# Token rows of 192 features instead of 256 columns, and a split that writes low parts to the other half of the partitions

## The chip, the cores and the metric

One core of one Trainium2 chip runs the whole program in one launch. The metric is the device time of the launch in microseconds (us), lower is better. All instructions of the five engines (TensorE or PE, VectorE or DVE, ScalarE or ACT, GpSimd or POOL, SyncE or SP) are placed by hand, and waits are semaphores that the program sets itself.

## The reference

A small language-model tower in float32: 8 sequences of 256 tokens, 192 features per token. An embedding with layer norm, four transformer layers with banded attention, then four residual blocks on normed input. Cut to its core:

```python
def layer_norm(x, s, b): ...
for l in range(4):
    q = heads(h @ Wq[l] + bq[l]); k = heads(h @ Wk[l] + bk[l]); v = heads(h @ Wv[l] + bv[l])
    a = band_attention(q, k, v, mask)          # each token sees 64 tokens to either side
    h = layer_norm(h + a @ Wo[l] + bo[l], ln1_s[l], ln1_b[l])
    f = gelu(h @ W1[l] + b1[l])                # 192 -> 768
    h = layer_norm(h + f @ W2[l] + b2[l], ln2_s[l], ln2_b[l])
h = h + channel_attention(layernorm(h))        # 8 heads of 24 channels, softmax over channels
h = h + best_expert_of_4(layernorm(h))         # argmax gate, each expert 192 -> 768 -> 192
h = h + full_attention(layernorm(h))           # 12 heads, 8 x 256 tokens
h = h + best_2_of_8_experts(layernorm(h))      # softmax over the two best scores
```

The output is h, 2048 x 192. The attention mask is all ones in these inputs, and there are 2048 tokens = 16 tiles of 128.

## The kernel before

**Tiles.** A token tile is 128 tokens, one per partition. `h` (the residual stream) and `xn` (normed or attention rows) are `[128, 16, 256]`: columns 0 to 191 are the features, and columns 192 to 255 hold features 128 to 191 a second time. The 16 tiles go in four groups of four (`GT = 4`). `hb` holds h plus the next bias, 192 wide.

**Turn and split.** Each product contracts over features, so a tile's features have to lie on partitions. PE transposes a tile in two turns of 128 columns (`pe_transpose`, L431; L1446 for the experts, L2098 for the gates). The second turn therefore has features 128 to 191 twice: on partitions 0 to 63 and again on 64 to 127. A value is carried as a rounded part (fp32r) and the rest, its low part. ACT copies both turns rounded into `xx[:, 0:2]` (`act_split`, L652; L1502). DVE then makes the low parts (`dve_split`; the same pair stands at L1539/L1540):

```python
nc.vector.tensor_tensor(xx[:, 2, tk], ps[:, 0:P], xx[:, 0, tk].bitcast(F32), ALU.subtract)       # L765
nc.vector.scalar_tensor_tensor(xx[:, 1, tk], in0=xx[:, 1, tk].bitcast(F32), scalar=lo_rows[:, :],
                               in1=ps[:, P:2 * P], op0=ALU.mult, op1=ALU.add)                     # L766
```

`lo_rows` is 0 on partitions 0 to 63 and -1 on 64 to 127. So L766 puts the unrounded turn on the lower half of `xx[:, 1]` (where the output's rounding makes it the high part) and turns the upper half into low parts. It ends the split and lets PE go on (`xx_ready`). The weights match: `second` has rows 128 to 191 of the weights on both halves, `second_lo` their low parts on partitions 0 to 63 and zeros above. A product is five matmuls (`pe_features` L449 to L453, `pe_tokens` L459 to L463, the experts' L1459 to L1463).

**Who writes rows.** DVE writes h at the end of each layer norm: as two instructions per tile, 128 columns each, since columns 128 to 255 are features 128 to 191 written twice (`dve_affine` L938 and L941 after L932; `dve_norm_step` L854 and L857 after L848, which is the same norm cut into steps that stand between the pairs of the attention loop). `dve_normalise` (L912) writes `xn` in two instructions per tile, 192 and 64 wide. POOL's `pool_scale` writes attention rows and, on every other call, a copy of 64 columns (L1044). The experts read rows of `x_rows` in DRAM, 256 wide, by an indirect transfer (L1386) into `rows_in`, a piece of the `xn` buffer.

**Order of the work.** 0 to 62 us: loads, embedding gather, first norm. Then four layers of an attention part (96 pairs of heads: scores on PE, maximum L792 on DVE, exponentials L685 on ACT, transposes L563 on PE, high part L698 on ACT, low part L799 on DVE, values L584 to L586 on PE) and a tail (output product, norm, 192 to 768 to 192, norm), whose end overlaps with the next layer's opening. Then channel attention (1080 to 1201), gates (1201 to 1236), 11 expert tiles of 256 slots (to 1346), sums and norm (to 1380), full attention (1400 to 1545), tail and router (to 1642), 23 expert tiles (to 1840), last sums and output. DVE's order in a loop is fixed by `dve_step` and `dve_attention`, in a tail by `dve_tail` and the table `TURNED`.

Of the kernel before, what the change touches and what calls it, by code (L numbers as in the profile page):

```python
# [119 lines left out]
def build_tower(nc, a, out, stop=None):  # L120
    ctx = ExitStack()
    with ctx:
# [9 lines left out]
        columns = sb("columns", [P, 3])  # L132
        lo_rows, q_scale, neg_in = columns[:, 0:1], columns[:, 1:2], columns[:, 2:3]
# [41 lines left out]
        def over(n, *dims):  # L175
# [21 lines left out]
        early = [flat(xn[:, 8 + 3 * j:11 + 3 * j, :], "p a n -> p (a n)").bitcast(BF16)  # L197
                 .rearrange("p (a n) -> p a n", a=3) for j in range(2)] + [pieces[2]]
        spare = flat(xn[:, :, :], "p t d -> p (t d)")
        raw_e = [spare[:, 2 * FF * j:2 * FF * (j + 1)].rearrange("p (a n) -> p a n", a=2) for j in range(2)]  # L200
        rows_in = spare[:, 4 * FF:4 * FF + 4 * 256].rearrange("p (s n) -> p s n", s=4)
# [59 lines left out]
        padded = sig("weight_rows_padded", base=0)  # L261
# [88 lines left out]
        x_rows = nc.dram_tensor("x_rows", (NT * P, 256), F32, kind="Internal").ap()  # L350
# [73 lines left out]

        def pe_transpose(pe, it, s, t, src, ready, turn, n, inside=False):

            pe.wait_ge(ready.sem, ready.at(turn, n))
            pe.wait_ge(xx_ready.sem, xx_ready.at(it, s if inside else s - 1))
            o = turn_at(t, inside)
            for c in range(2):  # L430
                last = nc.tensor.transpose(o[:, c * P:c * P + P],  # L431
                                           src[:, t, c * P:c * P + P], ident[:, :])
            last.then_inc(xt_done.sem, 1)
# [308 lines left out]
        def dve_step(dve, ch, it, p, banded, tile):  # L742

            if p and step(p - 1, banded):
# [3 lines left out]
                elif kind == "tile":  # L748
                    tile(a, True)
                elif kind == "att":  # L750
                    dve_split(dve, it, turned(1, a), a, True)
                elif kind == "out":
                    dve.wait_ge(hb_ready.sem, hb_ready.at(it, normed(2, a) - 2 * NT))
                    dve.wait_ge(o_done.sem, o_done.at(it, a + 1))
                    nc.vector.tensor_tensor(h[:, a, 0:D], bank[BM[0]][:, 0:D], hb[:, a, :], ALU.add)\
                        .then_inc(o_read.sem, 1)
# [5 lines left out]
        def dve_split(dve, it, s, t, inside=False):  # L762
# [3 lines left out]
            nc.vector.scalar_tensor_tensor(xx[:, 1, tk], in0=xx[:, 1, tk].bitcast(F32), scalar=lo_rows[:, :],  # L766
                                           in1=ps[:, P:2 * P], op0=ALU.mult, op1=ALU.add)\
# [70 lines left out]
        def dve_norm_step(dve, ch, it, i, n, g, w):  # L838
# [8 lines left out]
            if i % 2 == 0:  # L847
                last_mark[0] = ch.mark(nc.vector.scalar_tensor_tensor(  # L848
                    hb[:, t, :], in0=h[:, t, 0:D], scalar=mv[:, t, 0:1], in1=ln_s[:, w, :],
                    op0=ALU.subtract, op1=ALU.mult))  # L850
            else:
                twice = lambda x: x.unsqueeze(1).to_broadcast([P, 2, D2])
# [22 lines left out]
        def dve_residual(dve, ch, it, half, g, hb_n=None):  # L875

            for t in range(GT * g, GT * g + GT):
# [11 lines left out]
                nc.vector.tensor_tensor(h[:, t, 0:D], ps[:, 0:D], hb[:, t, :], ALU.add)\  # L889
                    .then_inc(read.sem, 1)  # L890

        def dve_stats(dve, ch, it, half, g, read):

            c = []
            for i in range(GT):
                if read:
                    dve.wait_ge(read.sem, read.at(it, GT * g + i + 1))
                c.append(ch.mark(nc.vector.bn_stats(stats[:, (GT * g + i + NT - GT) % NT, :], h[:, GT * g + i, 0:D])))
# [28 lines left out]
        def dve_affine(dve, ch, it, n, g, w):  # L927
# [3 lines left out]
            for t in range(GT * g, GT * g + GT):  # L931
                c.append(ch.mark(nc.vector.scalar_tensor_tensor(  # L932
                    hb[:, t, :], in0=h[:, t, 0:D], scalar=mv[:, t, 0:1], in1=ln_s[:, w, :],
                    op0=ALU.subtract, op1=ALU.mult)))
            twice = lambda x: x.unsqueeze(1).to_broadcast([P, 2, D2])
            for i, t in enumerate(range(GT * g, GT * g + GT)):
                ch.done(c[i])
                nc.vector.scalar_tensor_tensor(  # L938
                    h[:, t, 0:P], in0=hb[:, t, 0:P], scalar=rstd[:, t, 1:2], in1=ln_b[:, w, 0:P],
                    op0=ALU.mult, op1=ALU.add)  # L940
                nc.vector.scalar_tensor_tensor(  # L941
                    h[:, t, P:2 * P].rearrange("p (a n) -> p a n", a=2), in0=twice(hb[:, t, P:D]),
                    scalar=rstd[:, t, 1:2], in1=twice(ln_b[:, w, P:D]), op0=ALU.mult, op1=ALU.add)                    .then_inc(h_ready.sem, 1)
# [46 lines left out]
        def pool_hb(pool, it, n, g, row):  # L990
            for t in range(GT * g, GT * g + GT):
                pool.wait_ge(h_ready.sem, h_ready.at(it, n + t % GT))
                nc.gpsimd.tensor_tensor(hb[:, t, :], h[:, t, 0:D], row[:, :], ALU.add)\
# [28 lines left out]
        def pool_weights(ch, w, c1, c0=0):  # L1022
# [7 lines left out]
            return nc.gpsimd.tensor_tensor(second_lo[0:D2, 0:c1], raw[0:D2, 1, c],  # L1030
                                           second[0:D2, 0:c1].bitcast(F32), ALU.subtract)

        def pool_scale(pool, it, f):
# [9 lines left out]
            if half:  # L1043
                last = nc.gpsimd.tensor_tensor(o[:, :, HEADS:, :], x[:, :, 2:6, :], r[:, :, 2:6, :], ALU.mult)  # L1044
# [234 lines left out]
        def dve_xc_out(dve, b):  # L1279
            dve.wait_ge(xc_o_done.sem, xc_o_done.at(0, b + 1))  # L1280
            for i in range(2):
                t = 2 * b + i
                dve.wait_ge(hb_ready.sem, hb_ready.at(LAYERS, normed(2, t) - 2 * NT))
                nc.vector.tensor_tensor(h[:, t, 0:D], bank[2][:, i * D:i * D + D], hb[:, t, :], ALU.add)\
# [151 lines left out]
        def pe_tiles(pe, m):  # L1436
            first, end = span(m)[0], span(m)[-1] + 1

            def turn(G):

                pe.wait_ge(e_rows_in[G % 2].sem, 32 * (G // 2 + 1))
                for s in range(2):
                    if G > first:
                        pe.wait_ge(e_x_ready.sem, 2 * G + s - 1)
                    for c in range(2):
                        last = nc.tensor.transpose(bank[BX[s]][:, c * P:c * P + P],  # L1446
                                                   rows_in[:, 2 * (G % 2) + s, c * P:c * P + P], ident[:, :])
                    last.then_inc(e_turned.sem, 1)
# [74 lines left out]
        def dve_tiles(dve, m):  # L1523
            first, end = span(m)[0], span(m)[-1] + 1

            def low(G, i):

                dve.wait_ge(e_hi_ready.sem, 2 * G + i + 1)
                rows = slice(0, P if i == 0 else D2)
                hi, lo, second, second_lo = (wa, wb)[G % 2]  # L1530
                nc.vector.tensor_tensor((lo, second_lo)[i][rows, 0:FF], raw_e[G % 2][rows, i, :],
                                        (hi, second)[i][rows, 0:FF].bitcast(F32), ALU.subtract)\
                    .then_inc(e_lo_ready.sem, 1)

            def split(G):
                for s in range(2):
# [3 lines left out]
                    nc.vector.scalar_tensor_tensor(xx[:, 1, tk], in0=xx[:, 1, tk].bitcast(F32), scalar=lo_rows[:, :],  # L1540
                                                   in1=ps[:, P:2 * P], op0=ALU.mult, op1=ALU.add)\
# [84 lines left out]
        def _(sp):  # L1626
            for dst, src in ((ident, "ident"), (lo_rows, "lo_rows"), (q_scale, "q_scale"),
# [9 lines left out]
            sp.dma_start(xn[:, 0:8, :].bitcast(I32), a["mask_BS_i1_0"].unsqueeze(0).to_broadcast([P, B, S]))\  # L1637
# [75 lines left out]
            if stop is None:  # L1713
                o = out.rearrange("(t p) d -> p t d", p=P)
                for g in range(NG):
                    tg = slice(GT * g, GT * g + GT)
                    sp.wait_ge(sum_ready.sem, sum_ready.at(0, g + 2))
                    sp.dma_start(o[:, tg, :], h[:, tg, 0:D]).then_inc(out_done.sem, 16)
                sp.wait_ge(out_done.sem, 16 * NG)
            if stop == "tok":  # L1720
                sp.wait_ge(h_ready.sem, h_ready.at(L, 0))
                sp.dma_start(out.rearrange("(t p) d -> p t d", p=P), h[:, :, 0:D]).then_inc(out_done.sem, 16)
# [3 lines left out]
        def _(pool):  # L1726
# [8 lines left out]
            for t in range(NT):  # L1735
                pool.indirect_dma_start(out=h[:, t, 0:D], out_offset=None, in_=a["L0_tok_emb_word"],
# [3 lines left out]
            pool.wait_ge(const_in.sem, 16 * 8)  # L1740
# [81 lines left out]
            for g in range(NG):  # L1822
# [3 lines left out]
                if g == 0:  # L1826
                    pool.wait_ge(rows_bo.sem, rows_bo.at(L + 1, 16))
                    pool.wait_ge(sum_ready.sem, sum_ready.at(0, 1))
                    for t in range(NT):
                        nc.gpsimd.tensor_tensor(hb[:, t, :], h[:, t, 0:D], row_bo[:, :], ALU.add)\  # L1830
# [13 lines left out]
        def _(act):  # L1844
            for s in (xh_ready, qf_ready, exp_done, pad_ready, hi_ready, f_ready, xc_qk_ready, xc_v_ready, xc_e_ready, xc_y_ready, r_ready, g2_exp):
                s.start(act)
            act.wait_ge(const_in.sem, 16 * 8)
# [401 lines left out]
```

## Time and profile before

| | |
|---|---|
| device time, 3 runs | 1876.59, 1876.82, 1877.55 us (median 1876.82) |
| span of the profiled execution | 1874.5 us; 2.3 us of the median lie around it |
| mean granted TensorE clock | 0.895 of full speed |
| PE busy | 1483.1 us (79%), 13098 matmuls |
| DVE busy | 1247.8 us (67%), 3542 instructions |
| ACT busy | 977.2 us (52%), 2392 instructions |
| POOL busy | 808.0 us (43%), 1177 instructions |
| DMA | 178.26 MB in 144317 packets, 95 GB/s |

The profiled execution has no separate device time, so the time beside its span is the median of the three runs. A busy engine isn't necessarily the bound: the program passes through stages in which one engine after another ends last. The chain of waits, followed back from the last instruction, covers the time from 836 us to the end; before that the stages repeat (layers 1 to 3 run as layer 4 does).

### The profile page before, as it was taken

What the parts mean: (1) busy time and instruction counts of PE and PEld (TensorE: products, weight loads), DVE (VectorE), ACT (ScalarE), POOL (GpSimd) and SP (SyncE); (2) the same over time, 40 slices, a digit from 0 to 9 for tenths busy, and PEclk for the clock granted to TensorE, in tenths of its full rate; (3) what the DMA queues carried; (4) which work ended last, traced back from release to release, by engine and by line L of the source; (5) the groups of instructions that cost most, each with busy time, mean ns of one, the idle gap of its engine ahead of it and who ended that gap; (6) DMA issues with size and microseconds to landing.
All of it is one profiled execution on the core that took longest, in us unless ns stands there. A gap on an engine that the chain in (4) does not pass through costs nothing.

```text
span 1874.5 us, 42615 instructions
## 1 busy us (share of the span) xinstructions
PE 1483.1 (79%) x13098; PEld 1235.0 (66%) x13098; DVE 1247.8 (67%) x3542; ACT 977.2 (52%) x2392; POOL 808.0 (43%) x1177
## 2 busy tenths in 40 slices
PE   0589889798897997998988759759668887499992
PEld 0367678677676776776767648449646766389992
DVE  4788966788767888668896652433379896434344
ACT  0378733688434885348873223225348882155550
POOL 6577333684235762247733310124356521144440
PEclk9899989899899997999998968669869996599996
DMA  4666101743005550035610000147534511257765
GB/s 105 176 149 127 36 1 33 170 86 84 1 5 138 108 121 2 1 70 140 128 33 1 1 14 1 45 138 224 173 89 100 112 22 45 97 175 237 225 212 179
DMA packets 144317, 178.26 MB, mean 95 GB/s; under 512 B 22096, under 2 KB 106128, under 8 KB 143952
## 3 DMA queue, kind: packets, MB, share of 16 engines
q1 hardware_dynamic: 136784, 158.18, 32.9%
q0 software_dynamic: 7296, 17.18, 2.8%
q8 instruction: 117, 1.92, 0.5%
q14 instruction: 120, 0.98, 0.2%
HBM read 132.96 MB, written 42.34 MB: 94 GB/s over the span
## 4 chain that ended last, share of the span: by engine, by line
PE 31%; DVE 14%; issue 4%; DMA 2%; ACT 2%; POOL 2%; SPq 0%; DVEq 0%; POOLq 0%; ACTq 0%
PE bank L1473 7%; DVE ptl L799 4%; PE bank L1459 2%; DVE neg_max L792 2%; PE bank L645 1%; DVE xn L912 1%; PE bank L563 1%; PE bank L1460 1%; PE bank L1463 1%; PE bank L1461 1%; PE bank L1462 1%; PE bank L1217 1%; DMA xn<-y_rows 1%; PE bank L431 1%; PE bank L584 1%
## 5 line engine op out<-in xcount | busy, mean ns | idle before, releaser
L685 ACT ACTIVATE prob<-bank,neg_max 128x192 f32<-128x192 f32 (+1 forms) x960 | 406.9, 437 | 109.3 <-DVE neg_max L792 97.0
L792 DVE TENSOR_REDUCE neg_max<-bank 128x2 f32<-128x384 f32 (+1 forms) x480 | 274.3, 572 | 99.0 <-PE bank L544 91.4
L799 DVE TENSOR_TENSOR ptl<-bank,pth 128x384 f16<-128x384 f32 (+1 forms) x480 | 275.5, 574 | 4.6 <-ACT pth L698 4.0
L563 PE MATMUL bank<-ident,prob 128*128 128x128 f32 x1536 | 268.4, 288 | 0.0
L698 ACT ACTIVATE pth<-bank 128x384 f16<-128x384 f32 (+1 forms) x480 | 244.3, 509 | 9.3 <-PE bank L563 9.2
L652 ACT ACTIVATE xx<-bank 128x256 fp32r<-128x256 f32 x256 | 95.5, 386 | 196.0 <-PE bank L431 192.0
L544 PE MATMUL bank<-kx,qx 96*128 96x192 bf16 (+1 forms) x960 | 168.1, 257 | 1.1 <-DVE xx L766 1.1
L563 PEld LDWEIGHTS bank<-ident,prob 128*128 128x128 f32 x1536 | 162.9, 143 | 0.1
L584 PE MATMUL bank<-v,pth 128*128 128x33 bf16 x1152 | 138.4, 180 | 21.2 <-DVE ptl L799 18.0
L645 PE MATMUL bank<-w,fbuf 128*128 128x192 f32 x768 | 140.7, 327 | 2.0 <-DVE h L889 2.0
L734 ACT ACTIVATE fbuf<-bank,b 128x512 f32<-128x512 f32 x96 | 65.8, 687 | 146.5 <-PE bank L453 146.4
L542 PE MATMUL bank<-mask,ident 128*128 128x384 bf16 x384 | 130.6, 340 | 8.9 <-issue 7.3
L986 POOL TENSOR_SCALAR rstd<-mv 128x4 f32<-128x4 f32 x52 | 12.5, 240 | 289.4 <-DVE mv L902 283.4
L645 PEld LDWEIGHTS bank<-w,fbuf 128*128 128x128 f32 x768 | 128.6, 190 | 12.2 <-issue 5.2
L586 PE MATMUL bank<-v,ptl 128*128 128x33 bf16 x1152 | 136.5, 178 | 0.0
L585 PE MATMUL bank<-v,pth 128*128 128x16 bf16 x1152 | 132.9, 171 | 0.0
L584 PEld LDWEIGHTS bank<-v,pth 128*128 128x128 f16 x1152 | 99.4, 96 | 43.5 <-DVE ptl L799 42.8
L1396 POOL DMA_INDIRECT y_rows<-vf,mask x68 | 70.9, 1043 | 131.9 <-DVE vf L1550 116.0
L431 PE MATMUL bank<-ident,h 128*128 128x128 f32 x256 | 53.6, 315 | 83.8 <-DVE h L941 48.9
L544 PEld LDWEIGHTS bank<-kx,qx 96*128 96x128 bf16 x960 | 95.2, 101 | 36.0 <-issue 4.6
L1473 PE MATMUL bank<-w,fbuf 128*128 128x192 f32 x552 | 112.9, 329 | 0.0
L1515 ACT ACTIVATE fbuf<-bank,b 128x256 f32<-128x256 f32 x138 | 64.0, 473 | 89.4 <-PE bank L1463 60.4
(295 smaller groups left out, 4522.5 us busy)
## 6 DMA issues: line engine op xcount, KB each, us to landing
xn<-in_e_seg SPq DMA_DIRECT2D x34, 768.0 KB
w<-in_e_w SPq DMA_DIRECT2D x23, 576.0 KB
qk_rows<-fbuf SPq DMA_DIRECT2D x128, 96.0 KB, 2.3
qx<-qk_rows SPq DMA_DIRECT2D x35, 288.0 KB, 4.0
kx<-qk_rows SPq DMA_DIRECT2D x35, 288.0 KB, 5.8
qk_rows<-w SPq DMA_DIRECT2D x80, 96.0 KB, 2.3
qx<-qk_rows SPq DMA_DIRECT2D x35, 192.0 KB, 4.6
kx<-qk_rows SPq DMA_DIRECT2D x35, 192.0 KB, 5.2
```

Source lines behind the costliest of these rows:

```text
L542: nc.tensor.matmul(o, ident_bf, mask[:, 2 * b:2 * b + 2, :], start=True, stop=False)
L544: last = nc.tensor.matmul(o[:, qt, :], qx[0:ROWS, b % 3, hd, qt * P:qt * P + P], kx[0:ROWS, b % 3, hd, keys(qt, banded)], start=not banded ...
L563: last = nc.tensor.transpose(bank[BT[p % 2]][:, c * P:c * P + P], probs_at(p, banded, c * P, P), ident[:, :])
L584: nc.tensor.matmul(o, pth[:, p % 3, w], v[sums], start=first, stop=False)
L585: nc.tensor.matmul(o[third], pth[:, p % 3, w], v[lows], start=False, stop=False)
L586: return nc.tensor.matmul(o, ptl[:, p % 2, w], v[sums], start=False, stop=stop)
L645: last = nc.tensor.matmul(bank[BY[t]][:, 0:D], fbuf[:, (n - 2) % 4, t * P:t * P + P], w2[:, c, :], start=(c == 0), stop=(c == FC - 1))
L685: nc.scalar.activation(probs_at(p, banded, qt * n, n), scores_at(p, n)[:, qt, :], ACT.Exp, bias=neg_max[:, b % 2, hd, qt:qt + 1], scale=1. ...
L698: nc.scalar.activation(pth[:, p % 3, 0:n], bank[BT[p % 2]][:, 0:n], ACT.Copy).then_inc(hi_ready.sem, 1)
L792: nc.vector.tensor_reduce(neg_max[:, b % 2, hd, :], scores_at(p, D if banded else S), AX.X, ALU.max, negate=True).then_inc(max_ready.sem, 1)
L799: nc.vector.tensor_tensor(ptl[:, p % 2, 0:n], bank[BT[p % 2]][:, 0:n], pth[:, p % 3, 0:n], ALU.subtract)\
L1473: last = nc.tensor.matmul(bank[BY[2 * (G % 2) + s]][:, 0:D], fbuf[:, n % 4, s * P:s * P + P], w2_e[G % 3][:, c, :], start=(c == 0), stop=( ...
```

## The change

`h`, `xn`, `x_rows` and `rows_in` become 192 wide, without the second copy. The first turn takes columns 0 to 127 as before, the second columns 64 to 191, so that features 128 to 191 come out on partitions 64 to 127 (and features 64 to 127 on 0 to 63, unused). ACT rounds both turns as before. The split's second instruction subtracts on 64 partitions: it reads 64 to 127 and writes the low parts to partitions 0 to 63. `second_lo` then has low parts on all 128 partitions, so its zero rows and their two memsets go; so do `lo_rows` and its load. Norm outputs become one instruction of 192 columns per tile.

```diff
-        h = sb("h", [P, NT, 256])
-        xn = sb("xn", [P, NT, 256])
+        h = sb("h", [P, NT, D])
+        spare = sb("spare", [P, NT * 256])[:, :]
+        xn = spare[:, 0:NT * D].rearrange("p (t d) -> p t d", d=D)
...
-        x_rows = nc.dram_tensor("x_rows", (NT * P, 256), F32, kind="Internal").ap()
+        x_rows = nc.dram_tensor("x_rows", (NT * P, D), F32, kind="Internal").ap()
...
+        def turn_rows(o, rows):
+
+            nc.tensor.transpose(o[:, 0:P], rows[:, 0:P], ident[:, :])
+            return nc.tensor.transpose(o[:, P:2 * P], rows[:, D - P:D], ident[:, :])
...
             nc.vector.tensor_tensor(xx[:, 2, tk], ps[:, 0:P], xx[:, 0, tk].bitcast(F32), ALU.subtract)
-            nc.vector.scalar_tensor_tensor(xx[:, 1, tk], in0=xx[:, 1, tk].bitcast(F32), scalar=lo_rows[:, :],
-                                           in1=ps[:, P:2 * P], op0=ALU.mult, op1=ALU.add)\
+            nc.vector.tensor_tensor(xx[0:D2, 1, tk], ps[D2:P, P:2 * P], xx[D2:P, 1, tk].bitcast(F32), ALU.subtract)\
                 .then_inc(xx_ready.sem, 1)
...
-                nc.vector.scalar_tensor_tensor(
-                    h[:, t, 0:P], in0=hb[:, t, 0:P], scalar=rstd[:, t, 1:2], in1=ln_b[:, w, 0:P],
-                    op0=ALU.mult, op1=ALU.add)
-                nc.vector.scalar_tensor_tensor(
-                    h[:, t, P:2 * P].rearrange("p (a n) -> p a n", a=2), in0=twice(hb[:, t, P:D]),
-                    scalar=rstd[:, t, 1:2], in1=twice(ln_b[:, w, P:D]), op0=ALU.mult, op1=ALU.add)\
-                    .then_inc(h_ready.sem, 1)
+                nc.vector.scalar_tensor_tensor(
+                    h[:, t, :], in0=hb[:, t, :], scalar=rstd[:, t, 1:2], in1=ln_b[:, w, :],
+                    op0=ALU.mult, op1=ALU.add).then_inc(h_ready.sem, 1)
...
-                for dst, src in ((slice(0, D), slice(0, D)), (slice(D, 256), slice(P, D))):
-                    last = nc.vector.tensor_scalar(xn[:, t, dst], h[:, t, src], mv[:, t, 0:1],
-                                                   rstd[:, t, 1:2], ALU.subtract, ALU.mult)
-                last.then_inc(xn_ready.sem, 1)
+                nc.vector.tensor_scalar(xn[:, t, :], h[:, t, :], mv[:, t, 0:1],
+                                        rstd[:, t, 1:2], ALU.subtract, ALU.mult).then_inc(xn_ready.sem, 1)
...
-            return nc.gpsimd.tensor_tensor(second_lo[0:D2, 0:c1], raw[0:D2, 1, c],
-                                           second[0:D2, 0:c1].bitcast(F32), ALU.subtract)
+            return nc.gpsimd.tensor_tensor(second_lo[:, 0:c1], raw[:, 1, c],
+                                           second[:, 0:c1].bitcast(F32), ALU.subtract)
...
-            if half:
-                last = nc.gpsimd.tensor_tensor(o[:, :, HEADS:, :], x[:, :, 2:6, :], r[:, :, 2:6, :], ALU.mult)
...
-            for dst, src in ((ident, "ident"), (lo_rows, "lo_rows"), (q_scale, "q_scale"),
+            for dst, src in ((ident, "ident"), (q_scale, "q_scale"),
                              (neg_in, "neg_in"), (pad_keys, "pad_keys")):
                 sp.dma_start(dst[:, :], a[src]).then_inc(const_in.sem, 16)
...
-            nc.vector.memset(wa[3][D2:P, :].bitcast(F32), 0.0)
-            nc.vector.memset(wb[3][D2:P, :].bitcast(F32), 0.0).then_inc(padded.sem, 1)
```

The experts' turn, split and low parts (L1446, L1539/L1540, L1531) change in the same way, and the gates' product reads `wg[D2:P, 1]` in place of `wg[0:D2, 1]`. No wait of the kernel is moved; PE's instructions are as many as before. In the changed kernel the split's pair is L766/L767, the norm step's one instruction L853, the affine's L930, the normalise L906.

Two places on DVE show what is replaced. In the first attention loop (a norm step of the opening behind a split, between two pairs), before:

```order
L763 REGISTER_ALU
L765 TENSOR_TENSOR xx<-bank,xx 128x128
L766 SCALAR_TENSOR_TENSOR xx<-xx,columns,bank 128x128
L99 ISA
L854 SCALAR_TENSOR_TENSOR h<-hb,rstd,ln_b 128x128
L857 SCALAR_TENSOR_TENSOR h<-hb,rstd,ln_b 128x128
L791 REGISTER_ALU
L792 TENSOR_REDUCE neg_max<-bank 128x2
```

and now:

```order
L764 REGISTER_ALU
L766 TENSOR_TENSOR xx<-bank,xx 128x128
L767 TENSOR_TENSOR xx<-bank,xx 64x128
L99 ISA
L853 SCALAR_TENSOR_TENSOR h<-hb,rstd,ln_b 128x192
L791 REGISTER_ALU
L792 TENSOR_REDUCE neg_max<-bank 128x2
```

The place of the split and of the step is the same; the second instruction of the split has half the partitions, and the step is one instruction instead of two.

At the channel attention's input, where DVE makes statistics, normalises the second group of four tiles and splits the first, before (the pair L912 comes four times, once per tile):

```order
L902 BN_AGGR mv<-stats 128x2 x4
L912 TENSOR_SCALAR xn<-h,mv,rstd 128x192
L912 TENSOR_SCALAR xn<-h,mv,rstd 128x64
...
L765 TENSOR_TENSOR xx<-bank,xx 128x128
L766 SCALAR_TENSOR_TENSOR xx<-xx,columns,bank 128x128
```

and now:

```order
L897 BN_AGGR mv<-stats 128x2 x4
L906 TENSOR_SCALAR spare<-h,mv,rstd 128x192 x4
L766 TENSOR_TENSOR xx<-bank,xx 128x128
L767 TENSOR_TENSOR xx<-bank,xx 64x128
```

Four instructions stand where eight did, ahead of the same four splits.

## Rows read from the trace of the kernel before

**Rows 1.** Stages: stretch, length, busy PE, PEld, DVE, ACT, POOL, PEclk, DMA, GB/s.

```profile
850.00:975.00 125.00, 110.73 (x1437) 88.27 (x1433) 110.95 (x293) 104.33 (x295) 77.38 (x123) 0.99 0.45 96
975.00:1080.00 105.00, 83.22 (x464) 71.56 (x462) 69.17 (x252) 28.01 (x54) 33.77 (x54) 0.88 0.01 4
1080.00:1102.00 22.00, 9.04 (x32) 4.64 (x32) 17.97 (x78) 5.92 (x16) 3.91 (x6) 0.50 0.06 14
1346.00:1380.00 34.00, 8.72 (x28) 5.92 (x28) 25.76 (x84) 4.63 (x9) 9.68 (x15) 0.60 0.33 101
1642.00:1840.00 198.00, 193.06 (x1333) 182.35 (x1331) 78.45 (x185) 107.45 (x228) 88.86 (x87) 0.98 0.64 200
```

**Rows 2.** DVE by line and form: busy, mean ns; idle before, releaser.

```profile
L766 DVE SCALAR_TENSOR_TENSOR xx<-xx,columns,bank 128x128 fp32r<-128x128 f32 x256 | 86.5, 338 | 0.0
L765 DVE TENSOR_TENSOR xx<-bank,xx 128x128 fp32r<-128x128 f32 x256 | 73.2, 286 | 52.7 <-ACT xx L652 52.2
...
L912 DVE TENSOR_SCALAR xn<-h,mv,rstd 128x192 f32<-128x192 f32 x64 | 24.2, 379 | 0.6 <-POOL rstd L987 0.6
L912 DVE TENSOR_SCALAR xn<-h,mv,rstd 128x64 f32<-128x64 f32 x64 | 19.6, 307 | 0.0
...
L1531 DVE TENSOR_TENSOR wa_second_lo<-xn,wa_second 64x768 fp32r<-64x768 f32 x17 | 16.8, 986 | 6.3 <-issue 3.3 <-ACT wa_second L1495 3.0
...
L1531 DVE TENSOR_TENSOR wa_lo<-xn,wa_hi 128x768 fp32r<-128x768 f32 x17 | 16.3, 959 | 50.0 <-ACT wa_hi L1495 45.5 <-issue 4.5
```

**Rows 3.** Timeline of SP, first issues: start, length.

```profile
0.73 0.39 SPq L1629 DMA_DIRECT2D ident<-in_ident  x1
1.18 0.42 SPq L1629 DMA_DIRECT2D columns<-in_lo_rows  x1
```

**Rows 4.** Timeline of DVE, layer norm of a group, without and with POOL beside it.

```profile
264.06 1.41 DVE L932 SCALAR_TENSOR_TENSOR hb<-h,mv,ln_s 128x192 f32<-128x192 f32 x4 [1.69 <-POOL rstd L987]
...
267.05 0.68 DVE L941 SCALAR_TENSOR_TENSOR h<-hb,rstd,ln_b 128x128 f32<-128x128 f32 x1
...
267.91 0.68 DVE L941 SCALAR_TENSOR_TENSOR h<-hb,rstd,ln_b 128x128 f32<-128x128 f32 x1
...
277.47 0.35 DVE L938 SCALAR_TENSOR_TENSOR h<-hb,rstd,ln_b 128x128 f32<-128x128 f32 x1
277.74 0.35 DVE L941 SCALAR_TENSOR_TENSOR h<-hb,rstd,ln_b 128x128 f32<-128x128 f32 x1
```

**Rows 5.** Chain of waits, channel attention's input: start, length, what.

```profile
1080.02 2.14 DVE xn L912 x8
...
1085.56 0.20 DVE xx L765
1085.76 0.27 DVE xx L766
...
1086.86 0.39 ACT xx L652
...
1087.27 0.29 DVE xx L765
1087.57 0.25 DVE xx L766
```

**Rows 6.** Chain of waits, other stretches that the change touches.

```profile
845.65 0.34 DVE xx L766
...
974.34 0.26 DVE h L854
974.60 0.26 DVE h L857
...
1238.64 6.96 DMA xn<-x_rows,mask
...
1373.36 4.56 DVE xn L912 x16
...
1593.02 0.27 DVE xx L766
```

More of the change, by code:

```diff
@@ L429, in pe_transpose @@
             o = turn_at(t, inside)
[L430 to L433, printed above, removed]
+            turn_rows(o, src[:, t, :]).then_inc(xt_done.sem, 1)
         def pe_turn(pe, it, k, g, read):
@@ L888, in dve_residual @@
                     ps, read = bank[BY[t % 4]], y_read
-                nc.vector.tensor_tensor(h[:, t, 0:D], ps[:, 0:D], hb[:, t, :], ALU.add)\
+                nc.vector.tensor_tensor(h[:, t, :], ps[:, 0:D], hb[:, t, :], ALU.add)\
                     .then_inc(read.sem, 1)
@@ L992, in pool_hb @@
                 pool.wait_ge(h_ready.sem, h_ready.at(it, n + t % GT))
-                nc.gpsimd.tensor_tensor(hb[:, t, :], h[:, t, 0:D], row[:, :], ALU.add)\
+                nc.gpsimd.tensor_tensor(hb[:, t, :], h[:, t, :], row[:, :], ALU.add)\
                     .then_inc(hb_ready.sem, 1)
@@ L1444, in turn @@
                         pe.wait_ge(e_x_ready.sem, 2 * G + s - 1)
[L1445 to L1448, printed above, removed]
+                    turn_rows(bank[BX[s]], rows_in[:, 2 * (G % 2) + s, :]).then_inc(e_turned.sem, 1)
             def up(n):
@@ L1528, in low @@
                 dve.wait_ge(e_hi_ready.sem, 2 * G + i + 1)
-                rows = slice(0, P if i == 0 else D2)
                 hi, lo, second, second_lo = (wa, wb)[G % 2]
-                nc.vector.tensor_tensor((lo, second_lo)[i][rows, 0:FF], raw_e[G % 2][rows, i, :],
-                                        (hi, second)[i][rows, 0:FF].bitcast(F32), ALU.subtract)\
+                nc.vector.tensor_tensor((lo, second_lo)[i][:, 0:FF], raw_e[G % 2][:, i, :],
+                                        (hi, second)[i][:, 0:FF].bitcast(F32), ALU.subtract)\
                     .then_inc(e_lo_ready.sem, 1)
@@ L1829, in _ @@
                     for t in range(NT):
-                        nc.gpsimd.tensor_tensor(hb[:, t, :], h[:, t, 0:D], row_bo[:, :], ALU.add)\
+                        nc.gpsimd.tensor_tensor(hb[:, t, :], h[:, t, :], row_bo[:, :], ALU.add)\
                             .then_inc(hb_ready.sem, 1)
@@ L1846, in _ @@
                 s.start(act)
-            act.wait_ge(const_in.sem, 16 * 8)
+            act.wait_ge(const_in.sem, 16 * 7)
             def first_split(it):
@@ L1927, in _ @@
             dve.wait_ge(mask_in.sem, 32)
-            km = xn[:, 8:16, :]
-            ch.link(nc.vector.tensor_copy(km, xn[:, 0:8, :].bitcast(I32)))
-            ch.link(nc.vector.tensor_scalar(xn[:, 0:8, :], km, 0.0, -1.0, ALU.is_gt, ALU.add))
-            ch.link(nc.vector.tensor_scalar(km, xn[:, 0:8, :], -NEG_IN, None, ALU.mult))
+            km_in, km = [spare[:, j * B * S:(j + 1) * B * S].rearrange("p (b s) -> p b s", s=S) for j in range(2)]
+            ch.link(nc.vector.tensor_copy(km, km_in.bitcast(I32)))
+            ch.link(nc.vector.tensor_scalar(km_in, km, 0.0, -1.0, ALU.is_gt, ALU.add))
+            ch.link(nc.vector.tensor_scalar(km, km_in, -NEG_IN, None, ALU.mult))
             for t in range(NT):
@@ L1991, in _ @@
                     dve_merge(dve, ch, 0, g)
-                    added = ch.mark(nc.vector.tensor_tensor(h[:, tg, 0:D], h[:, tg, 0:D], hb[:, tg, :], ALU.add))
+                    added = ch.mark(nc.vector.tensor_tensor(h[:, tg, :], h[:, tg, :], hb[:, tg, :], ALU.add))
                 if g == NG:
@@ L2096, in _ @@
                             pe.wait_ge(gx_ready.sem, t - 1)
-                        for c in range(2):
-                            last = nc.tensor.transpose(bank[BX[t % 2]][:, c * P:c * P + P],
-                                                       xn[:, t, c * P:c * P + P], ident[:, :])
-                        last.then_inc(gx_done.sem, 1)
+                        turn_rows(bank[BX[t % 2]], xn[:, t, :]).then_inc(gx_done.sem, 1)
                 if g >= 2:
@@ L2170, in lay_out @@
     o["ident"] = np.eye(P, dtype=np.float32)
-    o["lo_rows"] = -(row >= 64).astype(np.float32)[:, None]
     o["q_scale"] = np.where(row < 64, DH ** -0.5, 1.0).astype(np.float32)[:, None]
```

56 lines of the change are left out of this document (24 added, 32 removed).

## The prediction

> **What bounds the kernel now.** I read the busy times by stage first, then VectorE's groups by line and form, then the chain of waits through the stretches that the change touches. The stages don't share one bound [rows 1]. In the experts' stretch PE is busy for 193.06 of 198 us: nothing that DVE or POOL saves there shows. In a layer's attention (850 to 975) PE has 110.73 of 125 us and DVE 110.95, and they hand work to each other in a ring, so what DVE saves counts in part. In a tail PE leads (83.22 of 105), with gaps at each turn. In the two norms without matrix work, 1080 to 1102 and 1346 to 1380, DVE is busy for 17.97 of 22 and 25.76 of 34 us and PE for 9: there nearly every DVE instruction lies on the path. So the change has to be costed as DVE time, stage by stage.
>
> Two views of DVE are to be kept apart. The mean of an instruction is from its start to its end; the next one starts before that end. The split's first instruction has a mean of 286 ns [rows 2], yet where it isn't held up its successor starts 0.20 us behind it, and the pair repeats after 0.20 + 0.26 = 0.46 us [rows 5]. Pitch, not mean, is what an instruction costs in a row of them; the mean counts only where someone waits for its end.
>
> **Terms that save.** All are against the profiled execution, which goes with the median of 1876.8 us.
>
> Start: one transfer fewer is issued by SP ahead of the token list. Issues stand 0.45 us apart (0.73 to 1.18) [rows 3], and the gather hangs on the token list. −0.5. The two memsets run while DVE waits for that list: 0.
>
> Normalise, 64 tiles: eight instructions for four tiles take 2.14 us on the chain [rows 5], so a tile costs 0.515 with the last one's end taken off. The 192-wide one is 379 − 307 = 72 ns longer than the 64-wide one [rows 2]; split so, the pitches are 0.295 and 0.22, and 0.22 us per tile go. Where they lie on the path: the channel attention's input, 16 tiles, −3.5. The gates' 16 tiles, −1.7, half of it, since after the second group PE and ACT's loop over the groups sets the pace. The norm of 1346 to 1380, −2.3: of the first two groups most is given back to a wait for PE's turn and ACT's copy, the last sixteen instructions (4.56 us) [rows 6] lose their eight at the end. Last tail, 8 of 16 tiles, −1.7. Sum −9.2.
>
> Norm output, first norm of the program: two 128-wide instructions cost 0.27 each (277.47, 277.74) [rows 4], one 192-wide of the same kind (1.41 − 0.09) / 4 = 0.33. So −0.20 per tile, twelve tiles not covered by statistics and POOL: −2.4. Where POOL adds the bias at the same time, a tile takes 0.86 us (267.05 to 267.91) [rows 4] and the saving may be larger.
>
> Norm steps in the attention loops: 32, each a pair of 0.26 us [rows 6], less 0.20 each. By the chain of layer 4 half of them are on the path: 16 × 0.20 = −3.2.
>
> Norms in tails: the last group of layer 4, where nothing else is left, −1.2 (4 × 0.30, between 0.20 and 0.40 with POOL beside). In the other groups DVE's saving comes before a turn by PE, and ACT's copy then holds it up; I take 0.15 of it for 12 groups, −1.8. Sum −3.0.
>
> Gather of the experts' rows, 1024 to 768 bytes each: the first gather of both expert stages is on the path, 6.96 us from issue to use [rows 6]. A quarter of it, for both, is −3.4 if it goes by bytes, 0 if by rows. These are 128 small rows, so I take near the lower end: −1.0.
>
> At no cost: POOL's copy of 64 columns (POOL isn't waited for there), PE (the same instructions and widths), ACT (the same). The experts' low parts get 128 instead of 64 partitions, and the 64-partition form is no quicker (986 against 959 ns) [rows 2]; PE is full there anyway [rows 1]. Sum of these terms: −19.3.
>
> **The split.** Its second instruction has the same 128 columns on half the partitions. [Rows 2] say that halving partitions saves nothing. It has the kind of the first (subtraction of two tensors) instead of three operands, so for itself its price is 286 ns and pitch 0.20, against 338 ns and 0.26. But it starts on partition 64, while its neighbours start on 0, and no DVE instruction of this kernel does that, so the trace has no price for it. The bounds: either it overlaps with its neighbours as L766 does, or it doesn't overlap with the one before and the one after. Without overlap the pair takes 0.286 + 0.286 = 0.57 us, against a pitch of 0.46 and an end 0.20 + 0.34 = 0.54 after its start.
>
> How many splits are on the path: in the chain from 836 us on L766 stands 50 times (845.65 the first, 1593.02 the last [rows 6]) and the experts' L1540 8 times; 20 of these lie in layer 4's attention and tail, so I add 60 for the layers ahead of it, 118 in all. By what follows them after 836: 12 stand alone between ACT and PE (the loop in [rows 5], 1086.86 to 1087.57) and pay 0.57 − 0.54 = 0.03; 14 are the second pair of two before PE and pay 0.10; 24 are followed by DVE and pay 0.11. That is 0.4 + 1.4 + 2.6 = 4.4, with 1.6 for each of three more layers and 0.5 in the opening +9.8. With overlap it is 118 × −0.055 = −6.5. I take the upper end, no overlap: an instruction whose partitions differ from its neighbours' has to read and write in another place, and nothing in the trace shows such a neighbour being overlapped. Both ends stay in the range.
>
> On this the Trainium skill has a rule, on the page "VectorE: DVE Perf Modes", section "Two Vector instructions with no wait between them": a Vector instruction whose input or output starts in another group of 32 partitions than the last one's is held until all earlier ones have finished. By that rule both the subtraction and the instruction behind it would be held, and the time would be 1867; without it 1851. No row here shows it, since all neighbours start on partition 0.
>
> Sum: −19.3 + 9.8 = −9.5, so 1876.8 − 9.5 = **1867.3 us**, 0.5% faster.
>
> **Rivals.**
> A, the split overlaps. For: 0.06 us of gap is what DVE needs between any two instructions of the trace, whatever their kind. Against: none of them changes partitions. Time: 1876.8 − 19.3 − 6.5 = 1851.0.
>
> B, the same time. The loops' ring and the turns are bound by PE and ACT, and DVE's savings only lengthen its waits: it stands idle for 52.7 us ahead of L765 for ACT already [rows 2]. Then of the normalises 5 us are left, of the first norm 1.2, of steps and tails 3.0, of start and gather 0.5, together 9.7, and the splits' +9.8 is paid in full: 1876.9. Against: in [rows 5] eight normalises in a row stand on the chain.
>
> C, slower: the subtraction across halves costs more than an instruction without overlap, since it reads one half and writes the other. At 0.2 us more per split (pair 0.77) it is 118 × 0.2 = 23.6 on top: 1890.9. The point from which it decides: 9.5 / 118 = 0.08 us more per split. For: no instruction of the trace does this, so nothing caps its price. Against: 64 partitions as such cost 27 ns at 768 columns [rows 2].
>
> That the change doesn't do what it says isn't a case: the order of instructions shows one for two in each norm.
>
> **How the numbers follow.** What a measurement of this kernel can tell from no change is 0.2%, 3.75 us. Chances: forecast 0.50, A 0.25, B 0.12, C 0.08, and 0.05 for larger savings than A's (path shares of the norms too low). The likeliest case alone runs from 1859 (gather by bytes, three quarters of the norm steps on the path) to 1873. The range goes from 1847, below A, to 1877, B's value. Outside are C and the edges of A and B, nearly 2 in 10. Faster 0.80, same 0.12, slower 0.08.
>
> **What would show it.** Right: DVE has some 210 instructions fewer; the new split starts its second instruction 0.29 us behind the first instead of 0.20, and what follows starts 0.29 later; four normalises take 1.3 us instead of 2.14; 1080 to 1102 is 2 to 3 us shorter; the experts' stretch keeps its 198 us. A is shown by a pitch of 0.20 in the pair, C by 0.37 or more. The forecast is wrong if the attention stages change by more than 2 us each, if the waits of ACT and PE around the turns grow by what DVE saved, or if the splits on the path are far from 118.

## The result, and the profile after

The changed kernel takes 1886.06 us (median of 9 runs, 1875.71 to 1897.91), beside 1876.28 us for the kernel before (9 runs, 1868.35 to 1877.74) on the same chips: a ratio of 1.0073, 95% interval 1.0052 to 1.0093. It is slower, by about 10 us. I had forecast 1867.3, and given slower a chance of 0.08. In a later session two of ten executions of the changed kernel, of 2689 and 2794 us, count as slow and are left out of its ratio; its median is 1887.27 with them and 1887.1 without.

The profiled execution is the longest of the nine (span 1896.1 us, clock 0.889); its second profile below has a span of 1885.7. Stretches of the profile after that answer to [rows 1], shifted to where the same work stands (columns as there):

```profile
857.00:982.00 125.00, 109.36 (x1390) 87.75 (x1388) 108.55 (x279) 101.46 (x285) 74.41 (x116) 0.96 0.43 93
1089.60:1109.00 19.40, 10.02 (x32) 4.76 (x32) 15.72 (x61) 5.75 (x15) 3.87 (x6) 0.50 0.07 16
```

The norm at the channel attention's input has 61 DVE instructions instead of 78, and its stretch is 19.4 us instead of 22. On the chain of waits, from the first normalise to the last turn, it is 19.6 instead of 21.8, so 2.2 us less. So the saving is there. But the program as a whole is longer. VectorE by line and form, answering to [rows 2]:

```profile
L767 DVE TENSOR_TENSOR xx<-bank,xx 64x128 fp32r<-64x128 f32 x256 | 75.0, 293 | 3.4
L766 DVE TENSOR_TENSOR xx<-bank,xx 128x128 fp32r<-128x128 f32 x256 | 74.0, 289 | 62.0 <-ACT xx L653 58.8
...
L906 DVE TENSOR_SCALAR spare<-h,mv,rstd 128x192 f32<-128x192 f32 x64 | 20.0, 376 | 2.1 <-POOL rstd L976 1.9
```

By this view the split got cheaper: 293 ns for its second instruction against 338. The mean of one instruction hides the cost, and only the starts show it. In an attention loop, the timeline of DVE before:

```profile
962.30 0.28 DVE L765 TENSOR_TENSOR xx<-bank,xx 128x128 fp32r<-128x128 f32 x1
962.50 0.34 DVE L766 SCALAR_TENSOR_TENSOR xx<-xx,columns,bank 128x128 fp32r<-128x128 f32 x1
962.75 0.55 DVE L792 TENSOR_REDUCE neg_max<-bank 128x2 f32<-128x384 f32 x1
963.22 0.55 DVE L799 TENSOR_TENSOR ptl<-bank,pth 128x384 f16<-128x384 f32 x1
```

and the same place after:

```profile
969.63 0.28 DVE L766 TENSOR_TENSOR xx<-bank,xx 128x128 fp32r<-128x128 f32 x1
969.93 0.29 DVE L767 TENSOR_TENSOR xx<-bank,xx 64x128 fp32r<-64x128 f32 x1
970.25 0.56 DVE L792 TENSOR_REDUCE neg_max<-bank 128x2 f32<-128x384 f32 x1
970.84 0.56 DVE L799 TENSOR_TENSOR ptl<-bank,pth 128x384 f16<-128x384 f32 x1
```

From the start of the split to the start of L799 it is 0.92 us before and 1.21 after. Three gaps grew: first to second instruction of the split 0.20 to 0.30, second to the maximum L792 0.25 to 0.32, and L792 to L799 0.47 to 0.59. The third I hadn't thought of. L792 reads PSUM alone; L799 is the first instruction after the split that reads SBUF, at partition 0, where the last one to read SBUF had started on 64. Over all splits of the two profiles the medians are the same: 0.202 to 0.305; from the second instruction to whatever follows 0.255 to 0.325 (0.324 where L792 follows); and for the 37 splits that stand ahead of an L792 with an L799 behind it 0.468 to 0.590.

### The profile page after: what moved, and what is told of

It reads as the page before. It is cut to its first block, busy times and chain, and to the rows that moved or that the text cites. A ratio compares the mean times of both kernels' runs of the same rounds, so it can differ in the third digit from the quotient of the medians.

```text
span 1896.1 us, 42364 instructions
## 1 busy us (share of the span) xinstructions
PE 1495.4 (79%) x13098; PEld 1240.4 (65%) x13098; DVE 1234.4 (65%) x3332; ACT 980.3 (52%) x2392; POOL 787.8 (42%) x1137
## 4 chain that ended last, share of the span: by engine, by line
PE 30%; DVE 14%; issue 6%; DMA 2%; ACT 2%; POOL 2%; SPq 0%; DVEq 0%; POOLq 0%; ACTq 0%
PE bank L1457 5%; DVE ptl L799 3%; PE bank L646 2%; DVE neg_max L792 2%; PE bank L1443 2%; PE bank L564 1%; PE bank L426 1%; DMA spare<-y_rows 1%; PE bank L1447 1%; PE bank L1444 1%; PE bank L1204 1%; PE bank L1446 1%; PE bank L1445 1%; PE bank L585 1%; PE bank L427 1%
## 5 line engine op out<-in xcount | busy, mean ns | idle before, releaser
L792 DVE TENSOR_REDUCE neg_max<-bank 128x2 f32<-128x384 f32 (+1 forms) x480 | 275.0, 574 | 102.3 <-PE bank L545 96.0
L799 DVE TENSOR_TENSOR ptl<-bank,pth 128x384 f16<-128x384 f32 (+1 forms) x480 | 276.7, 576 | 6.3 <-ACT pth L699 3.7
L585 PE MATMUL bank<-v,pth 128*128 128x33 bf16 x1152 | 138.5, 180 | 23.0 <-DVE ptl L799 19.6
L426 PE MATMUL bank<-ident,spare 128*128 128x128 f32 x212 | 68.1, 332 | 86.1 <-DVE spare L906 35.2
L766 DVE TENSOR_TENSOR xx<-bank,xx 128x128 fp32r<-128x128 f32 x256 | 74.0, 289 | 62.0 <-ACT xx L653 58.8
```

The costliest lines, as they stand in the source:

```text
L585: nc.tensor.matmul(o, pth[:, p % 3, w], v[sums], start=first, stop=False)
L792: nc.vector.tensor_reduce(neg_max[:, b % 2, hd, :], scores_at(p, D if banded else S), AX.X, ALU.max, negate=True).then_inc(max_ready.sem, 1)
L799: nc.vector.tensor_tensor(ptl[:, p % 2, 0:n], bank[BT[p % 2]][:, 0:n], pth[:, p % 3, 0:n], ALU.subtract)\
```

## The experiments

My theory after the result: the rows save what I worked out, and the split's second instruction costs about twice what I took for it, because it starts on partition 64. The rivals: crossing from one half to the other is what costs; the narrow rows cost something themselves; the loss is TensorE's clock. Each kernel's ratio is to the kernel before in the same session.

**The split alone.** The kernel before, its rows 256 wide, with

```diff
-nc.vector.scalar_tensor_tensor(xx[:, 1, tk], in0=xx[:, 1, tk].bitcast(F32), scalar=lo_rows[:, :],
-                               in1=ps[:, P:2 * P], op0=ALU.mult, op1=ALU.add)
+nc.vector.tensor_tensor(xx[0:D2, 1, tk], ps[D2:P, P:2 * P], xx[D2:P, 1, tk].bitcast(F32), ALU.subtract)
```

at both places, and the low weights on all 128 partitions.

> The kernel before with the split's second instruction alone replaced: 64 partitions, reads 64 to 127, writes low parts to 0 to 63 (the low weights on all 128 partitions with it, the rows stay 256 wide). If the split is what costs (no overlap on either side, each of the pair 0.31 us instead of 0.20 and 0.26), it is slower than the kernel before by 15 to 30 us, about 1895, with +3 to +4 us in each layer. If the 192-wide rows or the narrow gathers cost, it stays within 4 us of the kernel before. If most of the loss is TensorE's clock in the gates and the router, which DVE's faster norms brought on, the splits add about +10 and those two stages keep their length.

Measured: 1905.29 us against 1873.29, ratio 1.0172 (1.0153 to 1.0191), so +32.0. The split by itself costs more than three times the whole loss of the change. The narrow rows don't cost; beside it the changed kernel is shorter, and that is what the rows save. The two medians are of different sessions, so I take each against the kernel before of its own: +9.8 (or +13.2 in the later session) less +32.0 leaves −22.2 or −18.8 us for everything that the change saves.

**The same on partitions 0 to 63.** The kernel before with

```diff
+nc.vector.tensor_tensor(xx[0:D2, 1, tk], ps[0:D2, P:2 * P], xx[0:D2, 1, tk].bitcast(F32), ALU.subtract)
```

in the same places. With rows 256 wide features 128 to 191 stand on both halves, so this makes the low parts on the lower half, without any numbers lost.

> The kernel before with the split's second instruction on partitions 0 to 63 in place (low parts where the doubled rows have features 128 to 191 a first time; high parts stay on 64 to 127), the low weights on all 128. Same result, same 64 partitions and same operation as in the change, but every partition range starts at 0. If the start partition or the crossing is what costs, the pair has a pitch of 0.20 + 0.20 us and the time is 3 to 7 us below the kernel before, about 1871. If half the partitions or the plain subtraction cost anything, it is as slow as the crossing one.

Measured: 1857.16 us against 1873.29, ratio 0.9915 (0.9893 to 0.9936), −16.1. That is more than I expected of it, and 48 us below the variant that reads from 64, which has the same instruction on as many partitions. DVE's timeline, channel attention's input:

```profile
1077.78 0.29 DVE L764 TENSOR_TENSOR xx<-bank,xx 128x128 fp32r<-128x128 f32 x1 [0.86 <-ACT xx L651]
1077.99 0.27 DVE L765 TENSOR_TENSOR xx<-bank,xx 64x128 fp32r<-64x128 f32 x1
1078.20 0.29 DVE L764 TENSOR_TENSOR xx<-bank,xx 128x128 fp32r<-128x128 f32 x1
1078.41 0.27 DVE L765 TENSOR_TENSOR xx<-bank,xx 64x128 fp32r<-64x128 f32 x1
```

Every start is 0.21 behind the last.

**The start without the crossing.** The changed kernel with its second instruction in place on the upper half:

```diff
-nc.vector.tensor_tensor(xx[0:D2, 1, tk], ps[D2:P, P:2 * P], xx[D2:P, 1, tk].bitcast(F32), ALU.subtract)
+nc.vector.tensor_tensor(xx[D2:P, 1, tk], ps[D2:P, P:2 * P], xx[D2:P, 1, tk].bitcast(F32), ALU.subtract)
```

> The changed kernel with its split's second instruction in place on partitions 64 to 127 (low parts stand where the high parts of features 128 to 191 were, high parts of features 64 to 127 stay on 0 to 63, so the products lack the high parts of the last 64 features and carry others). Nothing crosses, but the instruction starts on partition 64 among neighbours that start on 0. If the start partition is what stops the overlap, it is as slow as the changed kernel (about 1886) with the same 0.31 us pitches; if crossing from one half to the other is what costs, it is as quick as the variant on partitions 0 to 63.

Measured: 1884.18 us against 1873.29, ratio 1.0052 (1.0032 to 1.0073): near the changed kernel's ratios of 1.0073 and 1.0064, with intervals that overlap, and 47 us above the variant on partitions 0 to 63 below. This kernel leaves out the high parts of the last 64 features, so it is read for its time alone. Its timeline at the same place:

```profile
1094.26 0.29 DVE L766 TENSOR_TENSOR xx<-bank,xx 128x128 fp32r<-128x128 f32 x1 [0.63 <-ACT xx L653]
1094.57 0.29 DVE L767 TENSOR_TENSOR xx<-bank,xx 64x128 fp32r<-64x128 f32 x1
1094.89 0.29 DVE L766 TENSOR_TENSOR xx<-bank,xx 128x128 fp32r<-128x128 f32 x1
1095.20 0.29 DVE L767 TENSOR_TENSOR xx<-bank,xx 64x128 fp32r<-64x128 f32 x1
```

0.31 to 0.32 from start to start, and nothing crosses. So it is the start partition that differs from the neighbour's, and crossing is free beside it.

**The rows without the start on 64.** The changed kernel with the same instruction on partitions 0 to 63:

```diff
+nc.vector.tensor_tensor(xx[0:D2, 1, tk], ps[0:D2, P:2 * P], xx[0:D2, 1, tk].bitcast(F32), ALU.subtract)
```

> The changed kernel with its split's second instruction reading and writing partitions 0 to 63 (it makes low parts of features 64 to 127 instead of 128 to 191, so the products lack the low parts of the last 64 features and carry others in their place). It has all of the change's savings and no instruction that starts on partition 64. If the rows save what I worked out and only the split costs: 1876 - 19 - 6 = 1851. If the savings are hidden behind PE and ACT: 1870 or more. If the clock is lost because the norms are shorter, the gates stage is still 8 us longer than before at a granted clock of 0.5.

Measured: 1837.20 us against 1873.29, ratio 0.9817 (0.9794 to 0.9841), −36.1. Beside the variant with 256-wide rows and the same split (1857.16), measured in the same session, the rows are worth 20.0 us; with the crossing split on both sides it was 18.8 or 22.2.

**What the variants share.** The kernel before with the low weights on 128 partitions and without the memsets:

```diff
-            return nc.gpsimd.tensor_tensor(second_lo[0:D2, 0:c1], raw[0:D2, 1, c],
-                                           second[0:D2, 0:c1].bitcast(F32), ALU.subtract)
+            return nc.gpsimd.tensor_tensor(second_lo[:, 0:c1], raw[:, 1, c],
+                                           second[:, 0:c1].bitcast(F32), ALU.subtract)
...
-            nc.vector.memset(wa[3][D2:P, :].bitcast(F32), 0.0)
-            nc.vector.memset(wb[3][D2:P, :].bitcast(F32), 0.0).then_inc(padded.sem, 1)
```

> The kernel before, split untouched, with what the other variants of it share: the low weights of the second segment on all 128 partitions and the two memsets at the start gone. If these are next to nothing, it is 2 to 3 us faster than the kernel before (the gather can start earlier), so 1871, and the 16 us of the variant on partitions 0 to 63 come from its subtraction being 0.06 us shorter at nearly all 324 splits. If the weights' form is what sped up the experts (7.7 of the 16 us), it is 10 us faster, about 1863.

Measured: 1875.93 us against 1874.06, ratio 1.0013 (0.9995 to 1.0032). Its profile does gain 2.6 us by the first norm, but the median shows nothing. I had expected it 2 to 3 us faster, which is a miss. Against the kernel before of its own session it is +1.9 us, so −16.1 − 1.9 = −18.0 us belong to the split's subtraction on 0 to 63 alone, 0.056 us for each of 324. The weights' form isn't what sped up the experts either: their two stretches take 121.0 and 240.7 us here, against 120.5 and 241.4 before. Its two gaps are 0.207 + 0.198 (0.217 where another split follows) in place of 0.202 + 0.255, 0.03 to 0.05 us less, so 18.0 is somewhat more than the gaps alone give.

**Fewer changes of the start.** The changed kernel with the experts' splits of two tiles in the order first, first, second, second:

```diff
+                at = lambda s: slice(SLOT * (G % 2) + s * P, SLOT * (G % 2) + s * P + P)
                 for s in range(2):
...
                     nc.vector.tensor_tensor(xx[:, 2, tk], ps[:, 0:P], xx[:, 0, tk].bitcast(F32), ALU.subtract)
+                for s in range(2):
+                    tk, ps = at(s), bank[BX[s]]
                     nc.vector.tensor_tensor(xx[0:D2, 1, tk], ps[D2:P, P:2 * P], xx[D2:P, 1, tk].bitcast(F32), ALU.subtract)
```

> The changed kernel with the experts' splits written in another order: both tiles' first instructions, then both tiles' second ones (0, 0, 64, 64 in place of 0, 64, 0, 64). If a change of the start partition is what is paid, at each change, there are two instead of four per expert tile of 34: 68 times 0.10 us, of which the experts' stretches should show 3 to 7 us, so about 1880. If the price were one of each instruction that starts on 64, nothing changes there.

Measured: 1880.04 us against 1874.06, ratio 1.0030 (1.0011 to 1.0050); 7.2 us below the changed kernel of the same session. The two experts' stretches, from the first gather on, take 119.0 and 239.2 us, against 121.1 and 242.6 in the changed kernel's profile and 120.5 and 242.2 in its second one: 4.5 to 5.5 us less in all, as a price per change of the start gives; by a price per instruction they would have kept their length. DVE's timeline in one expert tile:

```profile
1705.41 0.56 DVE L1523 TENSOR_TENSOR xx<-bank,xx 128x128 fp32r<-128x128 f32 x2 [1.42 <-ACT xx L1486]
1705.99 0.50 DVE L1526 TENSOR_TENSOR xx<-bank,xx 64x128 fp32r<-64x128 f32 x2
```

The second pair lasts 0.50 us for two, so its members overlap: the second of them starts where the first did and isn't held.

**The changed kernel again**, for the clock.

> The changed kernel as it is, for a second profiled execution. If the 8.5 us that its first profile lost in the gates stage belong to that execution's clock and not to the change, the stretch from the last norm to the first gather takes about 27.8 us instead of 35.6 and the profiled execution comes out near 1886. If they belong to the change, it takes 35.6 us again.

Measured: 1887.27 us against 1874.06, ratio 1.0064 (1.0044 to 1.0084). The stretch from the last statistics of the gates' norm to the first gather takes 28.3 us in this profile, not 35.6. In the three variants of the changed kernel (on 0 to 63, in place, grouped order), which have the same norm, it is 27.8 to 27.9. So the loss there was one execution's clock. The chain of waits, the gates' product in the first profile of the changed kernel:

```profile
1233.92 1.80 PE bank L2085 x2
```

and in the second:

```profile
1227.93 0.95 PE bank L2085 x2
```

These are the engine's two levels, 1.2 and 2.4 GHz. The pairs of L2086 right behind them take 1.81 and 0.96. The granted clock of the whole stretch was 0.50 in the first:

```profile
1219.55:1255.17 35.62, 24.26 (x103) 7.56 (x101) 12.74 (x47) 8.52 (x18) 3.64 (x5) 0.50 0.23 71
```

0.74 in the second, and 0.75 before:

```profile
1210.00:1237.10 27.10, 15.29 (x101) 5.75 (x101) 14.42 (x55) 7.30 (x17) 2.91 (x4) 0.75 0.33 105
```

**Where the time lies.** Lengths in us between the starts of the same instructions (first score maximum of a layer or of the last attention, first statistics, first gather), worked out from the timelines; one profiled execution each:

| stretch | before | changed | split alone | on 0 to 63, rows 256 | on 0 to 63, rows 192 |
|---|---|---|---|---|---|
| start to first maximum | 81.6 | 79.3 | 80.6 | 79.2 | 77.4 |
| four layers | 995.3 | 1007.2 | 1016.7 | 988.3 | 978.6 |
| channel attention | 124.5 | 126.3 | 126.2 | 126.8 | 122.8 |
| gates | 35.7 | 42.4 | 35.7 | 35.3 | 34.7 |
| experts, first | 120.5 | 121.1 | 121.2 | 117.6 | 118.1 |
| norm to next maximum | 33.5 | 31.1 | 34.9 | 33.5 | 29.5 |
| attention | 162.9 | 165.0 | 163.9 | 162.7 | 163.5 |
| tail, router | 79.1 | 81.1 | 83.8 | 78.3 | 76.4 |
| experts, second, to the end | 241.4 | 242.6 | 242.6 | 233.7 | 232.3 |

The split alone loses 21.4 of its 31 us in the four layers. The variant on 0 to 63 gains 7.0 there and 10.6 in the two experts' stretches, where PE was busy for 193.06 of 198 us [rows 1] and I had written that nothing DVE saves would show.

In the experts' stretches the tiles follow each other in steps. The shortest step between two tiles' first splits goes with the length of a tile's split, from its first start to its last end:

| | split of a tile, us | shortest step, us |
|---|---|---|
| on 0 to 63, rows 256 | 0.875 | 8.000 |
| before | 1.003 | 8.125 |
| grouped order | 1.078 | 8.202 |
| split alone | 1.227 | 8.352 |

Each difference in the first column comes back in the second, within 0.003 us.

## Why the prediction was wrong

**The terms that save were right in their sum.** I had −19.3 us. The runs show −20.0 with the split on 0 to 63, and −18.8 or −22.2 with the crossing one. The pieces were off both ways, so the close sum is in part luck. Between the two variants on 0 to 63 [table above] the layers save 9.7 us (norm steps and tails, forecast 6.2), the norm before the last attention 4.0 (2.3), the channel attention 4.0 (3.5), the last tail 1.9 (1.7), but the start with the first norm 1.8 (2.9) and the gates 0.6 (1.7). Single pieces, from the profile after: four normalises stand in the chain with 1.25 and 1.14 us, where eight instructions took 2.14 [rows 5]; I had said 1.3.

```profile
1089.56 1.25 DVE spare L906 x4
...
1092.18 1.14 DVE spare L906 x4
```

The norm from 1346 on became 2.4 us shorter in all (33.5 to 31.1); that it looks like the forecast 2.3 is chance, since the split's loss of 1.4 is in it. The program's first norm became 3.1 us shorter from its first to its last statistics, and 2.3 in the second profile (forecast 2.4). The gather's wait went from 6.96 [rows 6] to 6.29 us:

```profile
1256.68 6.29 DMA spare<-x_rows,mask
```

0.7 and, at the second, 0.9 us; I had taken 1.0 for both.

**The term that failed is the split**, +9.8 forecast, +32.0 measured. I had its mechanism (no overlap with the instruction before and the one after) and its sign, missed a third instruction that is held, and had two sizes wrong. I had also written that no DVE instruction of the kernel before starts on partition 64. Two do, the memsets at 2.44 and 3.29 us (64 partitions, 64 to 127); but nothing follows the last of them for 3.9 us, so they gave no price.

First, the price of one. I took 0.57 us for the pair, the two means, against a pitch of 0.46. Measured, the second starts 0.305 after the first and what follows 0.324 after the second, 0.63 in all: a held instruction starts some 0.02 to 0.03 us after the end of the one it waits for. So where DVE goes on, it is +0.17 and not +0.11; and in the attention loops, where L792 and L799 follow, 0.12 more, at the first instruction that reads SBUF again. The Trainium skill has that one too, on the page "VectorE: DVE Perf Modes", section "Two Vector instructions with no wait between them": it keeps the last reader's start for SBUF and for PSUM apart. I had used the rule for two neighbours and not followed it to the third. By that L792, a reader of PSUM, is held, and L799, the next reader of SBUF, is held again; the trace agrees (0.324 and 0.590 us against 0.255 and 0.468).

Second, how many lie on the path. I counted 118 of 324, by the pieces L766 and L1540 in the chain of waits and a guess of 20 for each layer ahead of it. The two variants with 256-wide rows have the same instructions and differ in the start partition alone, so their difference measures the share. Where DVE goes on, their gaps differ by (0.305 − 0.207) + (0.324 − 0.217) = 0.21 us for a split, or 0.22 before another instruction (0.198). Where DVE waits behind the split, only the later start and end of the second instruction count, 0.12. Summed over the two timelines, outside the experts' stretches that could be 25.4 (first gap, 256 splits) + 23.9 (second gap, 188 splits with DVE going on) + 1.4 (the other 68) + 37 × 0.12 = 55.2 us. The measured difference there is 50.3 (the difference of the spans) − 12.5 (experts, table) = 37.8, so 0.68 of it counts, where I had 110 of 256 splits, 0.43. In the experts' stretches it could be 34 × (1.227 − 0.875) = 12.0 us, and 12.5 is measured: all of it counts, where I had 8 of 68. The steps say the same. For a layer alone: the crossing split loses 21.4 / 4 = 5.3 us, where I had 1.6 for each of three.

Why the count was low is argued, not shown. The chain names one instruction for each moment. In a ring where DVE, ACT and PE wait for each other in turn, an instruction that it doesn't name still delays the next one on its engine, and that one's reader. I had read that in a layer PE has 110.73 of 125 us and DVE 110.95 [rows 1], and there should have priced every DVE instruction and not the named ones. In the experts' stretches, with PE at 193.06 of 198 us, I had excluded any gain. The busy share didn't bear that: the same 1972 matmuls, at the same granted clock (0.88 and 0.90), are busy for 289.4 us before and for 281.0 in the variant on 0 to 63, so what this view calls busy isn't all work.

**The rivals.** C, slower, had the right sign and place by another mechanism: it put the loss on reading one half and writing the other, which the variant in place refutes, and its own sign, 0.37 us from first to second, didn't come (0.305). Its price was set on top of no overlap, and its decision point was 0.08 us more per split. With 118 splits and 9.5 us that is 0.163 for each in all, and what the splits cost came to 32.0 / 118 = 0.27 by that count. I gave it 0.08 because I had made it an extra mechanism, and had not asked what my own two numbers, the pair's 0.57 us and the 118, would do if each were off by half. A, that the split overlaps, is what the variants on 0 to 63 show: it needs equal starts. (The 0.06 us of gap that I gave for it isn't in the rows: the next instruction starts 0.08 us before the end, 0.286 against 0.202 and 0.338 against 0.255.) B, savings hidden, is refuted by the 20.0 us between the two variants on 0 to 63.

**What stays open.** The experts' stretches gain 10.6 us from splits that are 0.13 us shorter for a tile (1.003 to 0.875). By the shortest step (8.125 to 8.000) 34 tiles give 4.3. The rest is in the larger steps: in the kernel before, 14 of the 30 steps behind each stage's first take 8.55 to 8.66 us, in the variant none takes over 8.23. With the crossing split 7 take 8.62 to 8.71; with fewer of them it loses only 1.9 us there beside the kernel before, though its shortest step is 0.23 longer. What causes a larger step no run separates. Whether a shorter norm makes the low clock in the gates more frequent isn't settled either: of five profiles with it one had the low clock throughout, of four without it none.

**A faster version.** The kernel before with its subtraction on partitions 0 to 63 beats both: 1857.16 us, 0.9915 of before. It keeps 256-wide rows, since on 192 wide rows no window of 128 features puts the last 64 on the lower half as well. The 1837.20 of the other variant shows what would be had if one did; it isn't the same computation.

## What to carry to other kernels

Keep the start partition the same from one VectorE instruction to the next: a half-width instruction on the upper half delays itself and up to two behind it. Beside the same instruction on the lower half that is 0.10 to 0.13 us each here. Beside the instruction that it replaced its own mean even goes down (338 to 293 ns). Price such an edit by start-to-start gaps and not by means, and in a ring of engines that are all nearly full don't count only the instructions that the chain of waits names: here two thirds of the delay counted in the rest of the program and all of it in the experts' stretches, where the chain had given 0.43 and 8 of 68. An instruction with three operands is worth replacing by one with two when it stands in every turn (0.255 to 0.20 us here).

## What the runs showed of the hardware that I had not expected

- Two VectorE instructions with different start partitions don't overlap, in either direction (this much I had taken; the size and the next point not): 0.305 and 0.324 us from start to start, against 0.207 and 0.198 with equal starts, for the same 64-partition subtraction. Whether the output crosses halves makes no difference (0.304 and 0.325 in place).
- The delay reaches past an instruction that reads PSUM alone: the next reader of SBUF is 0.12 us late.
- Half the partitions don't make a subtraction quicker by themselves: 272 ns for 64 against 284 ns for 128 with equal starts.
- The same program has the gates' product at 0.95 or at 1.80 us per pair of matmuls, by the granted clock of that execution, 7.3 us of its time.
